# Attention and mixture of experts on one core: the orders of TensorE and ScalarE behind the last first scores, written out by hand

## The chip, the cores and the metric

The kernel runs on one core of a Trainium2 chip. The metric is the device time of one execution in microseconds (us), the lower the better. Before the change it is 196.55 us, the median of three runs (196.53 to 196.87).

## The reference

Eight sequences of 256 tokens with 128 features pass one block: attention with 16 heads of 8 features and a sliding window of 128 tokens, a residual and a layer norm, then a mixture of 8 experts of which each token uses its best two, a residual and a second layer norm.

```python
qkv = x @ w_qkv.T                        # x: (8, 256, 128); 16 heads, D = 8
att = einsum('bhqd,bhkd->bhqk', q, k) / sqrt(8)
att = where((j <= i) & (j >= i - 127), att, -inf); att = softmax(att)
out = einsum('bhqk,bhkd->bhqd', att, v) @ w_out.T
x1 = layernorm(x + out)
probs = softmax(x1 @ router_w); top_p, top_e = top_k(probs, 2)
y = sum over the two experts e of p_e * (gelu(x1 @ w_in[e] + b_in[e]) @ w_out[e] + b_out[e])
result = layernorm(x1 + y)
```

## The kernel before

Five engines each run a program of their own in order, and wait for one another by counting semaphores: a `wait_ge` stands ahead of the instruction that needs it, and everything behind it on that engine waits too.

**Attention.** Batch `b` (0 to 7) has 16 heads in 8 pairs. TensorE computes first scores (`scores`), from which VectorE takes the maximum of each row. The maxima are split in three bf16 parts, turned (`turn_max`), copied by ScalarE (`copy_max`) and put as extra rows under the stacked q by a DMA. Then TensorE computes the scores a second time, turned (keys on the partitions) and with the maximum subtracted: `turned_scores(b, p)` for pair `p`. ScalarE takes `exponentials(b, p)` of them, GpSimd masks two pairs (a quad `g`) at once with two selects (`mask_probs`, lines 443 and 445), and TensorE weighs the values with them (`weigh_values(b, g)`, called the product of quad g here). `turned_scores` has two places to write in turn (`pair_banks`), so a pair waits for the exponential of the pair before last. When four quads are done, ScalarE copies the output (`copy_output`), TensorE turns it (`turn_output`), VectorE divides by the sums (`normalise`), TensorE turns it back (`turn_attention`), ScalarE copies it (`copy_attention`), TensorE projects it (`project_out`), VectorE adds the residual and takes statistics, GpSimd makes the reciprocal deviation (`first_deviation`, lines 435 and 437), VectorE normalises (`first_norm`, line 770), and TensorE turns the result (`turn_x1`) and computes the router's logits (`route_logits`).

**What sets the order.** One loop over slots runs on each engine. In a slot each engine asks for every kind of work whether its turn has come (`batch_at(slot, offset)`, `pair_at`, `quad_at`). First scores end with slot 63 (`LAST_S1`); `turned_scores` lags them by 11 slots (`S2`), the products by 15 (`PV`). So slots 64 to 74 hold the turned scores of batch 6, pairs 5 to 7, and of batch 7. In these slots TensorE also issues `keep_warm(2, hid_bank[0])`, two products of zeros, 512 columns wide, that nobody reads: in slots 65 to 72, so 16 in all. VectorE has its own loop over the same slots, with this order behind the first scores: `normalise(5)`, `route_shift` (665), `split_weights` (784, 786), the residual, statistics and moments of batch 5, the routing of the first half of the tokens in stages (674 to 694) with `first_norm(5)` (770) in the middle, `split_x1(5)`, `normalise(6)` (743).

**Mixture of experts.** Tokens go in four chunks of 512. For each chunk and expert TensorE computes `first_layer(c, e)` (three products, 1173), ScalarE the gelu (`gelu`, 594), TensorE `second_layer(c, e)` (1187), and VectorE adds the share with its gate (860). `first_layer(0, 0)` stands in slot 73 already; gelu needs another activation table than the exponential, so ScalarE loads it between `exponentials(7, 7)` and `gelu(0, 0)`.

Of the kernel before, what the change touches and what calls it, by code (L numbers as in the profile page):

```python
# [12 lines left out]
B = 8  # L13
# [13 lines left out]
QUADS = H // 4  # L27
# [18 lines left out]
LAST_S1, LAST_S2 = 8 * B - 1, 8 * B - 1 + S2  # L46
# [34 lines left out]
def attention_moe(nc, x_t, x, wqkv_t, wout_t, router_w, w_in, b_in_t, w_out, b_out, out):  # L81
    scratch = nc.dram_tensor("scratch", [2, 2, ROWS, 2, PAIRS * T], BF16, kind="Internal").ap()

    with ExitStack() as ctx:  # L84
# [394 lines left out]
        def _(act):  # L479
# [71 lines left out]
            def route_exponentials(tiles, k):  # L551

                act.wait_ge(route_shifted, k)
                nc.scalar.activation(route[1][:, tiles, :], route[0][:, tiles, :], ACT.Exp).then_inc(route_exp, 1)
# [18 lines left out]
            for n in range(PICKED):  # L573
                take_even(n)

            for slot in range(LAST_S2 + 1):
                n = pair_at(slot)
                if n is not None:
                    exponentials(*n)
                for offset, piece in ((TURN_MAX, copy_max), (TURN_ATTN, copy_attention), (PROJECT_QK, take_top), (PROJECT_QK + 1, take_middle),  # L580
                                      (VALUES, pad_v), (COPY_O, copy_output), (TURN_X1, copy_x1), (LOGITS, copy_logits)):
                    b = batch_at(slot, offset)
                    if b is not None:
                        piece(b)
                if slot == LAST_S1 + 3:
                    route_exponentials(EARLY, 1)

            def gelu(c, e):

# [381 lines left out]
        def _(pe):  # L971
            mm = nc.tensor.matmul

            def keep_warm(count, bank=o_bank[:, :]):

                for _ in range(count):
                    mm(bank, idle_rows[:, 0:P], idle_rows[:, :], start=True, stop=True)
# [186 lines left out]
            def first_layer(c, e):  # L1164

                n = c * NX + e
                if n == 1:
                    pe.wait_ge(exp_done, B * PAIRS - 1)
                if n >= 2:
                    pe.wait_ge(gelu_done, n - 1)  # L1170
                cols = slice(c * CH, (c + 1) * CH)
                for i, (w, xx) in enumerate(((w_in_lo, x1_hi), (w_in_hi, x1_lo), (w_in_hi, x1_hi))):
                    last = mm(hid_bank[e % 2], w[:, e, :], xx[:, cols], start=i == 0, stop=i == 2)  # L1173
                last.then_inc(hid_ready, 1)
# [50 lines left out]
                pick_pair(n)  # L1225
            pe.wait_ge(consts_ready, 7)

            for slot in range(LAST_S2 + 1):
                n = pair_at(slot)
                if n is not None:  # L1230
                    turned_scores(*n)
                elif 0 < slot < S2:
                    keep_warm(2)
                n = jobs_at(slot)
                if n is not None:
                    scores(*n)

                b = batch_at(slot, TURN_MAX)
                if b is not None:
                    turn_max(b)  # L1240
                b = batch_at(slot, TURN_ATTN)
                if b is not None:
                    if b == 0:
                        pe.wait_ge(out_w_loaded, 16)
                    turn_attention(b)
                b = batch_at(slot, PROJECT_OUT)
                if b is not None:
                    project_out(b)
                b = batch_at(slot, PROJECT_QK)
                if b is not None:  # L1250
                    if b % 2 == 0:
                        pe.wait_ge(x_t_loaded[1 + b // 2], 16)
                    if b == 2:
                        pe.wait_ge(part_low, 2)
                    elif b < 5:
                        pe.wait_ge(max_copied, b - 2)
                    else:
                        pe.wait_ge(attn_copied, b - 4)
                    project_qk(b)
                b = batch_at(slot, VALUES)  # L1260
                if b is not None:
                    project_v(b)
                b = batch_at(slot, TURN_X1)
                if b is not None:
                    turn_x1(b)
                b = batch_at(slot, TURN_O)
                if b is not None:
                    turn_output(b)
                b = batch_at(slot, LOGITS)
                if b is not None:  # L1270
                    if b == 0:
                        pe.wait_ge(router_loaded, 16)
                    route_logits(b)
                n = quad_at(slot)
                if n is not None:
                    weigh_values(*n)
                b = batch_at(slot, PROJECT_QK + 1)
                if b is not None:
                    subtract_top(b)
                if slot > LAST_S1 + 1 and slot < LAST_S2 - 1:  # L1280
                    keep_warm(2, hid_bank[0])
                if slot == LAST_S2 - 1:
                    pe.wait_ge(w_lo_done, 1)
                    first_layer(0, 0)

            weigh_values(B - 1, QUADS - 2)
            first_layer(0, 1)
            second_layer(0, 0)
            weigh_values(B - 1, QUADS - 1)
            unit(0, 2)  # L1290
            turn_x1(B - 2)
            unit(0, 3)
# [71 lines left out]
```

## Time and profile before

| | |
|---|---|
| median of three runs | 196.55 us (196.53 to 196.87) |
| profiled execution | 196.5 us, of which the span of the trace 194.8 |
| TensorE busy | 169.4 us (87%) |
| VectorE busy | 154.8 us (79%) |
| ScalarE busy | 114.6 us (59%) |
| GpSimd busy | 84.1 us (43%) |
| granted TensorE clock, mean | 0.994 |

The profiled execution took 1.7 us more than its span, which is what lies around the first and the last instruction. Times in the trace count from the span's start. In its rows PE is TensorE (PEld its weight loads), DVE VectorE, ACT ScalarE, POOL GpSimd. A product's busy time goes on past the start of the next one, since they are pipelined; what a piece of work takes from TensorE is the distance from its start to the start of the next piece. The same holds for ScalarE and VectorE by some tens of ns. Slots 64 to 74 lie between 110.6 and 127.4 us.

### The profile page before, as it was taken

The numbers are of one execution on the slowest core, as the hardware profiler recorded it, in microseconds if no ns is written. First come the engines' busy times: TensorE is split into PE (matmuls) and PEld (weight loads), VectorE is DVE, ScalarE is ACT, GpSimd is POOL, SyncE is SP. The second block draws the span as 40 slices with busy tenths as digits, with TensorE's granted clock in tenths as the row PEclk, the third lists the DMA queues.
The fourth block names the chain that finished last, engine by engine and source line by source line (L and its number), as shares of the span: only waits on it lengthen the run. The fifth ranks groups of instructions, "written<-read, shape, count | busy, mean of one in ns | idle before, by whom it ended". The sixth has DMA issues, their size and how long they took to land. (4 is left out here: it accounts for less than half of the span.)

```text
span 194.8 us, 6184 instructions
## 1 busy us (share of the span) xinstructions
PE 169.4 (87%) x2450; PEld 121.5 (62%) x2460; DVE 154.8 (79%) x468; ACT 114.6 (59%) x216; POOL 84.1 (43%) x157
## 2 busy tenths in 40 slices
PE   7579887988989989889999899989999979999950
PEld 3354454655656656556656544558988869999950
DVE  6985959669598698697988999635798869898793
ACT  4542056687686766876857757564353784564720
POOL 7960006556563655746738366561043002603003
PEclk9999999999999999999999999999999999999997
DMA  5589594194780882955901000000000000020011
GB/s 142 148 232 222 168 242 132 53 212 125 158 226 11 176 206 72 214 160 110 218 13 57 2 8 0 3 0 0 5 0 0 3 27 27 0 59 0 3 53 54
DMA packets 23127, 17.25 MB, mean 89 GB/s; under 512 B 1827, under 2 KB 21179, under 8 KB 23099
## 3 DMA queue, kind: packets, MB, share of 16 engines
q1 hardware_dynamic: 23099, 16.87, 35.2%
q8 instruction: 19, 0.31, 0.7%
q14 instruction: 9, 0.07, 0.1%
HBM read 9.35 MB, written 7.34 MB: 86 GB/s over the span
## 5 line engine op out<-in xcount | busy, mean ns | idle before, releaser
L486 ACT ACTIVATE probs<-st 128x768 f32<-128x768 f32 x59 | 47.9, 811 | 23.8 <-PE st L1067 20.6
L443 POOL TENSOR_SCALAR_AFFINE_SELECT probs<-probs 128x1024 f32<-128x1024 f32 x32 | 35.1, 1097 | 57.4 <-ACT probs L486 57.3
L713 DVE TENSOR_REDUCE max_parts<-score_banks 128x2 f32<-128x384 f32 x64 | 32.6, 550 | 4.6 <-PE score_banks L1041 4.2
L594 ACT ACTIVATE hid<-score_banks,b_in_sb 128x512 f32<-128x512 f32 x32 | 21.9, 687 | 21.0 <-PE score_banks L1173 20.9
L716 DVE TENSOR_REDUCE max_parts<-score_banks 128x4 f32<-128x512 f32 x32 | 20.6, 686 | 13.6 <-PE score_banks L1041 13.6
L1067 PE MATMUL st<-stack 51*64 51x256 bf16 (+1 forms) x472 | 21.2, 254 | 6.2 <-ACT probs L486 5.7
L1030 PE MATMUL score_banks<-edges,ident_bf 64*64 64x256 bf16 (+1 forms) x192 | 19.0, 296 | 4.5 <-DVE max_parts L713 3.4
L1089 PE MATMUL o_bank<-probs,v 128*32 128x256 f32 x256 | 20.4, 391 | 0.0
L445 POOL TENSOR_SCALAR_AFFINE_SELECT probs<-probs 128x512 f32<-128x512 f32 x32 | 20.3, 634 | 0.0
L1067 PEld LDWEIGHTS st<-stack 51*64 51x64 bf16 (+1 forms) x472 | 8.6, 104 | 18.7 <-ACT probs L486 11.8
L860 DVE SCALAR_TENSOR_TENSOR x_rows<-st,gate,x_rows 128x128 f32<-128x128 f32 x64 | 18.1, 344 | 2.4 <-PE st L1187 2.0
L1041 PE MATMUL score_banks<-stack 48*64 48x192 bf16 (+2 forms) x512 | 19.1, 224 | 0.0
L1187 PEld LDWEIGHTS st<-w_out_sb,hid 128*128 128x128 f32 x128 | 16.6, 191 | 2.9 <-ACT hid L594 1.7
L1187 PE MATMUL st<-w_out_sb,hid 128*128 128x128 f32 x128 | 17.0, 276 | 1.3 <-ACT hid L594 1.3
L1173 PE MATMUL score_banks<-x_hi,w_in_lo 128*128 128x512 f32 x32 | 15.4, 480 | 0.0
L1030 PEld LDWEIGHTS score_banks<-edges,ident_bf 64*64 64x64 bf16 x192 | 7.5, 105 | 10.3 <-DVE max_parts L713 4.7
L1041 PEld LDWEIGHTS score_banks<-stack 48*64 48x64 bf16 x512 | 13.9, 107 | 0.0
L1091 PE MATMUL o_bank<-probs,v 128*32 128x128 f32 x256 | 12.9, 273 | 0.0
L1173 PE MATMUL score_banks<-x_hi,w_in_hi 128*128 128x512 f32 x32 | 12.6, 393 | 0.0
L1173 PE MATMUL score_banks<-x_lo,w_in_hi 128*128 128x512 f32 x32 | 12.6, 393 | 0.0
L468 POOL TENSOR_SCALAR var<-moments 128x2 f32<-128x2 f32 x8 | 1.7, 216 | 24.1 <-DVE moments L908 24.1
L1091 PEld LDWEIGHTS o_bank<-probs,v 128*32 128x32 f32 x256 | 8.3, 110 | 5.5
(136 smaller groups left out, 331.2 us busy)
## 6 DMA issues: line engine op xcount, KB each, us to landing
stack<-scratch SPq DMA_DIRECT2D x28, 192.0 KB, 4.0
scratch<-parts SPq DMA_DIRECT2D x16, 192.0 KB, 4.0
scratch<-parts SPq DMA_DIRECT2D x24, 128.0 KB, 3.8
x_rows<-x SPq DMA_DIRECT2D x4, 256.0 KB, 5.6
out<-y_sb SPq DMA_DIRECT2D x8, 128.0 KB, 1.8
x_t_sb<-x_t SPq DMA_DIRECT2D x3, 256.0 KB, 4.8
w_in_sb<-w_in SPq DMA_DIRECT2D x1, 512.0 KB, 5.8
w_out_sb<-w_out SPq DMA_DIRECT2D x1, 512.0 KB, 7.9
```

The costliest lines, as they stand in the source:

```text
L443: pool.affine_select(out=own, in_=own, compare_op=ALU.is_ge, fill=0.0, base=0, pattern=[[0, 2], [0, 4], [1, P]], channel_multiplier=-1).th ...
L486: nc.scalar.activation(probs[g][:, :, two, :].rearrange("p k j c -> p j k c"), pair_banks(PAIRS * b + p)[:, :, 0:3 * P].rearrange("p j (k ...
L594: nc.scalar.activation(hid[e % 2][:, :], hid_bank[e % 2], ACT.Gelu_apprx_tanh, bias=b_in_sb[:, e:e + 1]).then_inc(gelu_done, 1)
L713: nc.vector.tensor_reduce(top[:, 1, r, pair:pair + 2], bank[:, 0:384].rearrange("p (h c) -> p h c", h=2), X_AXIS, ALU.max, negate=True).th ...
L716: nc.vector.tensor_reduce(top[:, 0, r, pair:pair + 4], bank[:, :].rearrange("p (h c) -> p h c", h=4), X_AXIS, ALU.max, negate=True).then_i ...
L1030: mm(at, ident_bf[rows, 64 * r:64 * r + 64], mask, start=True, stop=True)
L1041: last = mm(bank[lo:lo + 64, i * width:i * width + keys.stop - keys.start], q[rows, pair + i, queries], k[rows, pair + i, keys], start=Fal ...
L1067: last = mm(to[cols, r, kt * T:kt * P + T], k[rows, p, at:at + 64], q[rows, p, kt * P:T], start=b > 0 or kt == 0, stop=b > 0, skip_group_c ...
L1089: last = mm(o_bank[rows, t * T:(t + 1) * T], v, probs[g][:, 0:2, j, :], start=s == 0, stop=s == 1, skip_group_check=True)
L1091: last = mm(o_bank[rows, t * T + P:(t + 1) * T], v, probs[g][:, 2, j, :], start=False, stop=s == 1, skip_group_check=True)
L1173: last = mm(hid_bank[e % 2], w[:, e, :], xx[:, cols], start=i == 0, stop=i == 2)
L1187: last = mm(y_bank[e % 4][:, i * E:(i + 1) * E], hid[e % 2][:, i * P:(i + 1) * P], w_out_sb[:, e, :], start=True, stop=True)
```

## The change

The loops of TensorE and of ScalarE end with slot 63, and the work of slots 64 to 74 stands written out, each call by hand. VectorE, GpSimd and the DMA queue keep their loops and their order. `late` is batch 6, `last` is batch 7.

```diff
--- before.py
+++ after.py
@@ -573,7 +573,7 @@
             for n in range(PICKED):
                 take_even(n)
 
-            for slot in range(LAST_S2 + 1):
+            for slot in range(LAST_S1 + 1):
                 n = pair_at(slot)
                 if n is not None:
                     exponentials(*n)
@@ -582,8 +582,27 @@
                     b = batch_at(slot, offset)
                     if b is not None:
                         piece(b)
-                if slot == LAST_S1 + 3:
-                    route_exponentials(EARLY, 1)
+
+            late, last = B - 2, B - 1
+            exponentials(late, 5)
+            copy_max(last)
+            exponentials(late, 6)
+            copy_attention(late - 1)
+            exponentials(late, 7)
+            route_exponentials(EARLY, 1)
+            exponentials(last, 0)
+            exponentials(last, 1)
+            pad_v(last)
+            copy_output(late)
+            exponentials(last, 2)
+            exponentials(last, 3)
+            copy_x1(late - 1)
+            exponentials(last, 4)
+            copy_logits(late - 1)
+            exponentials(last, 5)
+            copy_attention(late)
+            exponentials(last, 6)
+            exponentials(last, 7)
 
             def gelu(c, e):
 
@@ -1225,7 +1244,7 @@
                 pick_pair(n)
             pe.wait_ge(consts_ready, 7)
 
-            for slot in range(LAST_S2 + 1):
+            for slot in range(LAST_S1 + 1):
                 n = pair_at(slot)
                 if n is not None:
                     turned_scores(*n)
@@ -1277,16 +1296,40 @@
                 b = batch_at(slot, PROJECT_QK + 1)
                 if b is not None:
                     subtract_top(b)
-                if slot > LAST_S1 + 1 and slot < LAST_S2 - 1:
-                    keep_warm(2, hid_bank[0])
-                if slot == LAST_S2 - 1:
-                    pe.wait_ge(w_lo_done, 1)
-                    first_layer(0, 0)
-
-            weigh_values(B - 1, QUADS - 2)
+
+            late, last = B - 2, B - 1
+            turned_scores(late, 5)
+            turn_max(last)
+            turned_scores(late, 6)
+            weigh_values(late, 1)
+            turn_attention(late - 1)
+            turned_scores(late, 7)
+            weigh_values(late, 2)
+            project_out(late - 1)
+            keep_warm(2, hid_bank[0])
+            turned_scores(last, 0)
+            turned_scores(last, 1)
+            project_v(last)
+            weigh_values(late, 3)
+            turned_scores(last, 2)
+            turned_scores(last, 3)
+            turn_x1(late - 1)
+            turn_output(late)
+            turned_scores(last, 4)
+            route_logits(late - 1)
+            weigh_values(last, 0)
+            turned_scores(last, 5)
+            turn_attention(late)
+            turned_scores(last, 6)
+            weigh_values(last, 1)
+            project_out(late)
+            turned_scores(last, 7)
+            weigh_values(last, 2)
+            pe.wait_ge(w_lo_done, 1)
+            first_layer(0, 0)
             first_layer(0, 1)
             second_layer(0, 0)
-            weigh_values(B - 1, QUADS - 1)
+            weigh_values(last, 3)
             unit(0, 2)
             turn_x1(B - 2)
             unit(0, 3)
```

TensorE, at the turned scores of pairs 6 and 7 of batch 6 (1067 turned scores, 1138 `turn_attention(5)`, 1089 and 1091 the product of a quad, 977 the idle products, 1145 `project_out(5)`). Before:

```order
L1067 MATMUL score_banks<-stack 64x256 [waits maxima]
L1067 MATMUL score_banks<-stack 64x256 x3
L1067 MATMUL score_banks<-stack 64x128 x4
L1138 MATMUL misc<-ident,attn 128x128 [waits normed,max_copied]
L1138 MATMUL misc<-ident,attn 128x128
L1089 MATMUL o_bank<-probs,v 32x256 [waits masked]
L1089 MATMUL o_bank<-probs,v 32x256 x3
L1091 MATMUL o_bank<-probs,v 32x128 x4
L977 MATMUL score_banks<-idle_rows 128x512 x2
L1067 MATMUL st<-stack 64x256 [waits exp_done]
L1067 MATMUL st<-stack 64x256 x3
L1067 MATMUL st<-stack 64x128 x4
```

Now, with line numbers 19 higher:

```order
L1086 MATMUL score_banks<-stack 64x256 [waits maxima]
L1086 MATMUL score_banks<-stack 64x256 x3
L1086 MATMUL score_banks<-stack 64x128 x4
L1108 MATMUL o_bank<-probs,v 32x256 [waits masked]
L1108 MATMUL o_bank<-probs,v 32x256 x3
L1110 MATMUL o_bank<-probs,v 32x128 x4
L1157 MATMUL misc<-ident,attn 128x128 [waits normed,max_copied]
L1157 MATMUL misc<-ident,attn 128x128
L1086 MATMUL st<-stack 64x256 [waits exp_done]
L1086 MATMUL st<-stack 64x256 x3
L1086 MATMUL st<-stack 64x128 x4
L1108 MATMUL o_bank<-probs,v 32x256 [waits masked]
```

The product of quad 1 has moved ahead of `turn_attention(5)`, the turned scores of pair 7 stand ahead of the next product (of quad 2), and two pairs of idle products have become one.

TensorE, further on, from the turned scores of batch 7, pair 3 (1154 is `turn_x1(5)`, 1127 `turn_output(6)`, 1161 `route_logits(5)`). Before:

```order
L1067 MATMUL st<-stack 64x256 [waits exp_done]
L1067 MATMUL st<-stack 64x256 x3
L1067 MATMUL st<-stack 64x128 x4
L1154 MATMUL misc<-ident,x_rows 128x128 [waits x1_done]
L1154 MATMUL misc<-ident,x_rows 128x128
L977 MATMUL score_banks<-idle_rows 128x512 x2
L1067 MATMUL score_banks<-stack 64x256 [waits exp_done]
L1067 MATMUL score_banks<-stack 64x256 x3
L1067 MATMUL score_banks<-stack 64x128 x4
L1127 MATMUL misc<-ident,o_t 128x128 [waits o_copied,v_padded]
L1127 MATMUL misc<-ident,o_t 128x128 x3
L1161 MATMUL misc<-router_sb,x_t 128x8 [waits x1_copied]
```

Now:

```order
L1086 MATMUL st<-stack 64x256 [waits exp_done]
L1086 MATMUL st<-stack 64x256 x3
L1086 MATMUL st<-stack 64x128 x4
L1173 MATMUL misc<-ident,x_rows 128x128 [waits x1_done]
L1173 MATMUL misc<-ident,x_rows 128x128
L1146 MATMUL misc<-ident,o_t 128x128 [waits o_copied,v_padded]
L1146 MATMUL misc<-ident,o_t 128x128 x3
L1086 MATMUL score_banks<-stack 64x256 [waits exp_done]
L1086 MATMUL score_banks<-stack 64x256 x3
L1086 MATMUL score_banks<-stack 64x128 x4
L1180 MATMUL misc<-router_sb,x_t 128x8 [waits x1_copied]
L1180 MATMUL misc<-router_sb,x_t 128x8
```

`turn_output(6)` has moved from behind the turned scores of pair 4 to ahead of them, and the idle products have gone. Ahead of this piece the product of batch 6, quad 3, has moved in front of the turned scores of batch 7, pairs 2 and 3, which now stand back to back. Behind it `turn_attention(6)` moves from behind the turned scores of pair 6 to ahead of them, `project_out(6)` from behind those of pair 7 to ahead of them, and `first_layer(0, 0)` from ahead of them to behind the product of batch 7, quad 2.

On ScalarE two copies move: `copy_output(6)` from behind `exponentials(7, 3)` to ahead of `exponentials(7, 2)`, `copy_attention(6)` from behind `exponentials(7, 6)` to ahead of it. The routing's exponential (554) keeps its place behind `exponentials(6, 7)`.

## Rows read from the trace of the kernel before

**Rows 1.** Windows; after the window: its length, busy us and instructions by engine, clock, DMA:

```profile
115.00:125.00 10.00, 9.45 (x130) 4.63 (x130) 9.18 (x32) 6.29 (x15) 6.04 (x8) 1.00 0.00 0
130.40:188.00 57.60, 56.05 (x416) 50.55 (x416) 47.32 (x192) 32.36 (x56) 11.56 (x31) 1.00 0.04 13
188.00:194.80 6.80, 0.00 (x0) 0.00 (x0) 3.57 (x17) 0.00 (x0) 1.81 (x4) 0.83 0.20 57
```

**Rows 2.** Timeline of TensorE, 111 to 117: start, busy, line, tiles, [idle before]:

```profile
111.16 0.36 PE L1067 MATMUL score_banks<-stack 51*64 51x256 bf16 x8
112.20 0.44 PE L1138 MATMUL misc<-ident,attn 128*128 128x128 f32 x2 [0.68 <-ACT max_t L508]
112.56 0.64 PE L1089 MATMUL o_bank<-probs,v 128*32 128x256 f32 x8
...
113.89 0.36 PE L1067 MATMUL st<-stack 51*64 51x256 bf16 x8
...
115.54 0.64 PE L1089 MATMUL o_bank<-probs,v 128*32 128x256 f32 x8
...
116.33 0.60 PE L977 MATMUL score_banks<-idle_rows 128*128 128x512 bf16 x2
```

**Rows 3.** Timeline of ScalarE, the exponential of batch 6, pair 7:

```profile
114.30 0.81 ACT L486 ACTIVATE probs<-st 128x768 f32<-128x768 f32 x1 [1.18 <-PE st L1067]
```

**Rows 4.** Timeline of VectorE, 114 to 125:

```profile
114.20 1.22 DVE L786 TENSOR_TENSOR w_in_lo<-w_in_sb,w_in_hi 128x1024 fp32r<-128x1024 f32 x1
...
116.31 0.25 DVE L764 BATCH_NORM_AGGREGATE moments<-stats 128x2 f32<-128x6 f32 x2
...
118.26 1.07 DVE L678 TENSOR_TENSOR route<-route,row_stat 128x64 f32<-128x64 f32 x1
119.37 0.81 DVE L770 TENSOR_SCALAR x_rows<-resid,moments,rstd 128x128 f32<-128x128 f32 x2
...
121.37 0.93 DVE L678 TENSOR_TENSOR route<-route,row_stat 128x64 f32<-128x64 f32 x1
122.34 0.55 DVE L693 TENSOR_TENSOR route<-route 128x64 f32<-128x64 f32 x1
...
124.25 0.62 DVE L743 TENSOR_TENSOR attn<-misc,inv_sum 128x64 f32<-128x64 f32 x4
```

**Rows 5.** Timeline of GpSimd, 112 to 122:

```profile
112.98 0.64 POOL L445 TENSOR_SCALAR_AFFINE_SELECT probs<-probs 128x512 f32<-128x512 f32 x1
115.18 1.20 POOL L443 TENSOR_SCALAR_AFFINE_SELECT probs<-probs 128x1024 f32<-128x1024 f32 x1 [1.56 <-ACT probs L486]
...
116.94 0.21 POOL L435 TENSOR_SCALAR var_eps<-moments 128x2 f32<-128x2 f32 x1
117.23 0.70 POOL L437 TENSOR_TENSOR rstd<-var_eps,half_power 128x2 f32<-128x2 f32 x1
118.16 1.09 POOL L443 TENSOR_SCALAR_AFFINE_SELECT probs<-probs 128x1024 f32<-128x1024 f32 x1 [0.23 <-ACT probs L486]
...
121.13 1.09 POOL L443 TENSOR_SCALAR_AFFINE_SELECT probs<-probs 128x1024 f32<-128x1024 f32 x1 [1.29 <-ACT probs L486]
```

**Rows 6.** Lines 678 and 770 over the whole run; min/median/max ns of one:

```profile
L678 DVE TENSOR_TENSOR route<-route,row_stat x4: 217/578/1073, 118.3 to 161.2; 128x64 f32<-128x64 f32 x4
L770 DVE TENSOR_SCALAR x_rows<-resid,moments,rstd x16: 333/432/668, 55.1 to 143.3; 128x128 f32<-128x128 f32 x16
```

**Rows 7.** Timeline of TensorE, 125 to 131:

```profile
125.05 0.44 PE L1138 MATMUL misc<-ident,attn 128*128 128x128 f32 x2
...
127.10 0.36 PE L1067 MATMUL st<-stack 51*64 51x256 bf16 x8
127.39 0.71 PE L1145 MATMUL misc<-wout_sb,attn_t 128*128 128x128 f32 x4
...
130.38 1.16 PE L1187 MATMUL score_banks<-w_out_sb,hid 128*128 128x128 f32 x8 [0.60 <-ACT hid L594]
```

**Rows 8.** Timeline of TensorE at the start of the run:

```profile
1.24 3.60 PE L977 MATMUL o_bank<-idle_rows 128*128 128x512 bf16 x8 [1.24 <-DVE idle_rows L810]
```

## The prediction, as it stood before the changed kernel ran

> **What bounds the kernel now.** I read the windows first, for where each engine is busy [rows 1]. The reader is to see two regimes. From 130.40 to 188.00 TensorE is busy for 56.05 of 57.60 us: the mixture of experts runs at its pace, and behind it only the last norm and the store are left. So whatever moves the start of `second_layer(0, 0)` at 130.38 [rows 7] moves the end by as much. Ahead of it, from 115 to 125, TensorE is busy for 9.46 of 10 us, but VectorE too, for 9.18 [rows 1]. Part of TensorE's time are the idle products; VectorE has nothing of the kind.
>
> Then I read the timelines of that stretch, for what VectorE does there. It runs without a wait from 114.20 to the end of `normalise(6)` at 124.25 + 0.62 = 124.87 [rows 4]. `turn_attention(6)` on TensorE starts at 125.05 [rows 7], 0.18 behind it. Everything up to `second_layer(0, 0)` hangs on that one: 130.38 - 125.05 = 5.33 us of turned scores, a product, the last exponential, a table load and a gelu. So the pacer of the changed stretch is VectorE, with TensorE 0.1 us behind: a completion is seen some 0.07 us later (the exponential of [rows 3] ends at 115.11, the select behind it starts at 115.18 [rows 5]).
>
> Third, what VectorE's time is made of. Some of its instructions last longer than others of their line: 678 takes 0.217 us at the least and 1.073 at the most, 770 0.333 and 0.668 [rows 6]. The long ones lie under GpSimd's selects: 678 at 118.26 lasts until 119.33, the select at 118.16 until 119.25; 678 at 121.37 lasts until 122.30, the select at 121.13 until 122.22 [rows 4, 5]. Both end 0.08 behind it, which is less than their own 0.22: they wait until about 0.15 before the select's end and get in between its two halves. The costs from 115.42 to 124.87 are 0.85 and 0.71 (678), 0.55 - 0.22 = 0.33 (693), and 0.2 (770, whose pair takes 0.81 instead of 0.6): 2.1 us in all.
>
> **The change part by part.** (1) 14 of 16 idle products go. Two take at most 0.60 us [rows 2], so 14 take up to 4.2. If TensorE paced the stretch that would be the gain. It does not, so by itself this is worth the 0.18 - 0.07, some 0.12 us, that `turn_attention(6)` starts later than VectorE allows.
>
> (2) The turned scores of batch 6, pair 7, move from 113.89 [rows 2] to the front. Those of pair 6 start at 111.16 as before and take 0.29, the product of quad 1 takes 0.79 (115.54 to 116.33) and ends at 112.24, `turn_attention(5)` takes 0.36 (112.20 to 112.56) [rows 2], so they start at 112.60, 1.29 earlier. The exponential follows 0.41 later as now (113.89 to 114.30 [rows 2, 3]), at 113.0, and the select of quad 3 after it at 113.9 instead of 115.18 [rows 5]. It runs until 115.0.
>
> (3) That select now lies on `split_weights`. The difference of the weights (786), a 1024 wide operation with both inputs in SBUF like 678, starts at 114.20 and takes 1.22 [rows 4]; today the select comes when it is nearly done, and it is the select that lasts 1.20 instead of 1.09 [rows 5]. Now it finds the select running. By the behaviour of 678 it runs from 115.0 - 0.15 and ends at 116.1, against 115.42: 0.65 late. If the cast ahead of it (784, which ends where 786 starts) holds the select back, another 0.15. I take 0.7. Bounds: 0, if 786 doesn't wait as 678 does, and 1.4, if both halves of the select pass first (0.8, and 0.64 for the second half [rows 5]).
>
> No row here shows whether a cast can hold back a select. The Trainium skill (SBUF — State Buffer, section Who interferes with whom) says that a VectorE operation with two SBUF inputs, or a cast in a two-port mode, and a GpSimd operation that reads SBUF exclude each other for a whole instruction, whoever came first going on. By that rule the select starts at 114.1, 786 waits for its full end at 115.2 and ends at 116.4, and the sum below would be 197.3 instead of 197.0; the trace agrees on who waits, but its 678 ends only 0.08 behind the select.
>
> (4) VectorE's order behind it is unchanged, so statistics and moments of batch 5 end at 116.56 + 0.7 = 117.26 [rows 4]. GpSimd makes the deviation from them: 0.07, 0.30 (116.94 to 117.23) and 0.70 [rows 5], until 118.35. Then come the selects of batch 7. Its pairs 0 to 3 are ahead of time now (the select of quad 2 ends at 113.62 as now [rows 5]; its product 0.79, `project_out(5)` and two idle products bring the first two turned scores to 115.6 and 115.9, values and a product the next two to 117.9 and 118.2; with 0.41 to each exponential and 0.81 for it, and the copies of ScalarE between, the exponentials of pairs 1 and 3 are done at about 117.6 and 120.05), so quad 0 is selected from 118.4 to 120.1 and quad 1 right behind, from 120.15 to 121.85, instead of 118.16 and 121.13 [rows 5]. VectorE meets them with 676, 678 and the pair 770: 676 loses 0.85, 678 0.1, the first 770 0.8 (it starts just behind the begin of quad 1's select), the second 0.35. That is 2.1, as much as today, at other places; 678's second time, 693 and the split of x1 are clear of selects. `normalise(6)` ends 0.7 late, at 125.55.
>
> (5) TensorE meanwhile stands. `turn_x1(5)` needs the norm of line 770, which ends at 121.9, and the turned scores of pair 3 are issued by 118.5: 3.4 us without a product, where the idle products used to be. From there to the turned scores of pair 5 lie six pieces of work: two turned scores at 0.29, a product at 0.79, and three turns or projections, between 0.36 and 0.71 each by their nearest rows [rows 2, 7]: 2.5 to 3.5 us, done by 124.4 to 125.4. `turn_attention(6)` starts at 125.6, with `turn_output(6)` and the logits, moved ahead of it, hidden in VectorE's lateness (without that cover they cost up to 0.9).
>
> (6) Behind `turn_attention(6)` before: 0.36, product 0.79 and `first_layer(0, 0)` with the rest, 0.90, then the turned scores of pair 7, 127.10 - 125.05 = 2.05 us after it [rows 7]. Now: 0.36, turned scores of pair 6 0.29, product 0.79, `project_out(6)` up to 0.71 [rows 7]: 2.05 to 2.15. The same. `first_layer(0, 0)` and `(0, 1)`, 1.8 us, go behind the turned scores, under the last exponential and the table load, where TensorE waited 0.60 us [rows 7]; they fill that. The copies moved on ScalarE come ahead of exponentials that wait for TensorE anyway.
>
> **Sum.** 0.7 (786) + 0 (other meetings) - 0.12 (TensorE's lag) + 0 = 0.55 later at `second_layer(0, 0)`, and I take 0.5 for the cheap ends of the steps. The profiled execution took 196.5 us (194.8 and 1.7 around it), 0.05 under the median: 197.0 us. With 0.6 to 0.8 in (3) and 0.25 either way in (4), 196.75 to 197.4. Measurement tells a change from none at about 0.2%, 0.4 us.
>
> **The rivals.**
>
> *A, faster: VectorE escapes the selects.* What speaks for it: selects that come earlier may fall on reductions and on operations that read PSUM, which don't wait (the two moments at 116.31 took 0.25 although a select ran [rows 4, 5]). If none of 676, 678 and 770 waits, `normalise(6)` ends 2.1 earlier than in my sum, at 123.45, and the end comes 1.5 us earlier than today: 195.0. It is faster from the point where more than 0.6 of the 2.1 is saved. Against it: GpSimd works through quads 0 and 1 without a gap for 3.4 us, and all four instructions lie there. Chance 0.20, spread over 195.0 to 196.1.
>
> *B, no change: the delay is absorbed.* 786 is late but 0.3 to 0.6 comes back, since one select meets 677 instead of 676, or quad 1's select comes behind the pair 770 (it takes 0.3 us of lateness of its exponentials). 196.2 to 196.9. Chance 0.22.
>
> *C, my forecast*, 196.75 to 197.4, chance 0.48.
>
> *D, the clock falls.* TensorE stands for 3.4 us at 118.5 and works about half of the time around it. Today the granted clock is 1.00 from 115 to 188; after the last product, before 188.0, it stays up and falls only at about 192.5 (mean 0.83 over the last 6.8 us) [rows 1], over 4 us later. At the start of the run eight idle products take 3.60 us, 0.45 each, against 0.30 later [rows 2, 8]; that is the slow level of the clock, and it lasted that long. If it fell to 1.2 GHz at 121.9, the work of (5) and (6) would run at half speed for at least as long, which loses half of 3.6, 1.8 us, and TensorE has at most 1.2 us of waiting for VectorE there to pay from: 0.6 more than my forecast at the least, up to 2 if the clock comes back late: 197.6 to 199. Chance 0.10.
>
> The Trainium skill (TensorE: Matmul & The Clock Gate, section HAM oscillation — how this bites in real kernels) warns of just such gaps between bursts; no row of this trace shows a fall inside the run.
>
> **How the numbers follow.** Slower by over 0.2%: D, and C but for its lowest tenth, 0.54. Same: B with what falls between, 0.25. Faster: A and the low edge of B, 0.21. The range leaves out the far half of A and of D: 195.9 to 197.8.
>
> **What would show it.** In the changed profile: the select of batch 6, quad 3, at 113.9, and 786 lasting 1.9 us instead of 1.22 (right: step 3); two quads of selects back to back from 118.4 with 676 and 770 long; TensorE waiting for x_rows of line 770 some 3.4 us; `turn_attention(6)` waiting for VectorE, at 125.6; `second_layer(0, 0)` at 130.9; from there to the end 64.4 us as now. If 786 lasts 1.22, or `normalise(6)` ends before 124.9, the forecast is wrong on the fast side; a granted clock under 1.00 between 118 and 130 means D.

## The result, and the profile after

The changed kernel is slower: 200.09 us, the median of four runs (199.07 to 200.81), against 196.56 before (196.53 to 196.87). The ratio is 1.0172, with a 95% interval of 1.0126 to 1.0218. The profiled execution took 200.09 us, its span 198.3; the prediction was 197.0, at most 197.8.

The page of the changed kernel, busy tenths and the granted clock in 40 slices of 4.96 us:

```profile
PE   7589887989989989899988883999999979999960
...
DVE  6985958678698696897988999324889869998793
...
PEclk9999999999999999999999996589999999999997
```

The third row is what is new: the clock digits read 6, 5 and 8 in slices 25 to 27, where the page of the kernel before has a 9 in each. The windows, two us each, show when (columns as in [rows 1]: TensorE's busy us come first behind the length, and the clock is the third number from the right):

```profile
116.00:118.00 2.00, 1.48 (x28) 0.94 (x20) 1.83 (x10) 1.96 (x6) 1.19 (x3) 1.00 0.00 0
118.00:120.00 2.00, 0.57 (x21) 0.31 (x16) 1.86 (x5) 1.84 (x4) 2.00 (x3) 1.00 0.00 0
120.00:122.00 2.00, 0.00 (x0) 0.00 (x0) 1.96 (x4) 0.18 (x1) 1.85 (x3) 0.66 0.00 0
122.00:124.00 2.00, 1.94 (x15) 1.33 (x15) 1.73 (x10) 0.38 (x1) 0.00 (x0) 0.50 0.00 0
124.00:126.00 2.00, 2.00 (x20) 1.52 (x20) 1.60 (x8) 0.99 (x2) 0.00 (x0) 0.50 0.00 0
...
128.00:130.00 2.00, 2.00 (x21) 1.16 (x20) 0.00 (x0) 0.87 (x2) 1.53 (x2) 0.50 0.00 0
130.00:132.00 2.00, 2.00 (x28) 1.15 (x28) 1.16 (x5) 0.89 (x2) 0.03 (x1) 0.78 0.00 0
132.00:134.00 2.00, 1.45 (x7) 0.84 (x6) 0.00 (x0) 1.99 (x3) 1.92 (x4) 1.00 0.00 0
```

TensorE is busy for 0.57 us of 118 to 120 and for nothing of 120 to 122. The clock is 1.00 until then, 0.66 on the mean of 120 to 122, 0.50 until 130 and 0.78 in the next two: it fell at about 120.7 and came back at about 130.9, so for 10.2 us it was at the lower of its two levels, 1.2 instead of 2.4 GHz. It came back after TensorE had been busy for 8.8 us almost without a gap, from 122.06 on.

TensorE's timeline has the same story (`turn_x1(5)` is the row of 122.06, `turn_attention(6)` that of 126.85, the last turned scores 130.52, `second_layer(0, 0)` 133.96):

```profile
118.23 0.34 PE L1086 MATMUL st<-stack 51*64 51x256 bf16 x8
122.06 0.69 PE L1173 MATMUL misc<-ident,x_rows 128*128 128x128 f32 x2 [3.50 <-DVE x_rows L789]
...
126.85 0.69 PE L1157 MATMUL misc<-ident,attn 128*128 128x128 f32 x2
...
130.52 0.52 PE L1086 MATMUL st<-stack 51*64 51x256 bf16 x8
...
133.96 1.16 PE L1206 MATMUL score_banks<-w_out_sb,hid 128*128 128x128 f32 x8 [0.55 <-ACT hid L613]
```

`second_layer(0, 0)` comes at 133.96 instead of 130.38 [rows 7], 3.58 late, and the span is 3.5 longer: behind it nothing was gained or lost. The row at 122.06 waits 3.50 us for the norm; such a time in which TensorE has nothing to issue is called a stop below. VectorE's rows (805 is 786 of before, 695 is 676, 789 is 770, 762 is 743), from its timeline:

```profile
114.23 1.99 DVE L805 TENSOR_TENSOR w_in_lo<-w_in_sb,w_in_hi 128x1024 fp32r<-128x1024 f32 x1
...
118.51 1.15 DVE L695 TENSOR_TENSOR route<-route,rank_w 128x64 f32<-128x64 f32 x1
...
120.29 1.72 DVE L789 TENSOR_SCALAR x_rows<-resid,moments,rstd 128x128 f32<-128x128 f32 x2
...
125.05 0.61 DVE L762 TENSOR_TENSOR attn<-misc,inv_sum 128x64 f32<-128x64 f32 x4
```

GpSimd's timeline beside them, the last select of batch 6 and quads 0 and 1 of batch 7:

```profile
113.93 1.22 POOL L443 TENSOR_SCALAR_AFFINE_SELECT probs<-probs 128x1024 f32<-128x1024 f32 x1 [0.28 <-ACT probs L486]
...
118.50 1.09 POOL L443 TENSOR_SCALAR_AFFINE_SELECT probs<-probs 128x1024 f32<-128x1024 f32 x1
...
120.25 1.09 POOL L443 TENSOR_SCALAR_AFFINE_SELECT probs<-probs 128x1024 f32<-128x1024 f32 x1
```

The difference of the weights lasts 1.99 us instead of 1.22, under the select that starts at 113.93; the norm's pair lasts 1.72 instead of 0.81 [rows 4], under the selects from 118.50 to 121.9. `normalise(6)` ends at 125.05 + 0.61 = 125.66 instead of 124.87.

### The profile page after: what moved, and what is told of

Same layout as the page of the kernel before. It is cut to its first block and busy times, and to the rows that moved or that the text cites. A ratio compares the mean times of both kernels' runs of the same rounds, so it can differ in the third digit from the quotient of the medians.

```text
span 198.3 us, 6166 instructions
## 1 busy us (share of the span) xinstructions
PE 171.2 (86%) x2446; PEld 122.7 (62%) x2446; DVE 155.5 (78%) x468; ACT 114.3 (58%) x216; POOL 85.2 (43%) x157
## 5 line engine op out<-in xcount | busy, mean ns | idle before, releaser
L1108 PE MATMUL o_bank<-probs,v 128*32 128x256 f32 x256 | 21.3, 406 | 0.7 <-POOL probs L445 0.7
L445 POOL TENSOR_SCALAR_AFFINE_SELECT probs<-probs 128x512 f32<-128x512 f32 x32 | 21.3, 664 | 0.0
L1110 PE MATMUL o_bank<-probs,v 128*32 128x128 f32 x256 | 13.4, 282 | 0.0
```

What stands on the lines that cost most here:

```text
L445: pool.affine_select(out=other, in_=other, compare_op=ALU.is_gt, fill=0.0, base=0, pattern=[[0, 4], [-1, P]], channel_multiplier=1).then_i ...
L1108: last = mm(o_bank[rows, t * T:(t + 1) * T], v, probs[g][:, 0:2, j, :], start=s == 0, stop=s == 1, skip_group_check=True)
L1110: last = mm(o_bank[rows, t * T + P:(t + 1) * T], v, probs[g][:, 2, j, :], start=False, stop=s == 1, skip_group_check=True)
```

## The experiments

Two theories stood against each other at first. Theory 1: two costs add, VectorE's lateness (by the walk 0.55) and the fallen clock (the rest, 3.0). Theory 2: the new order itself costs the time, and the clock is a companion. A third question was what let the clock fall, the missing idle products alone (in any order) or the new order with them (theory 3).

A note on comparing traces. The runs of one kernel lie mostly in two groups some 0.6 us apart (17 runs of before: 196.5 to 196.9 and 197.0 to 197.2), and the traces start in two ways. The first projection shows it, here from TensorE's timeline of the changed kernel:

```profile
4.62 1.03 PE L1002 MATMUL misc<-x_t_sb,wqkv_sb 128*128 128x256 f32 x4
```

And the same row of e1_fill:

```profile
4.62 1.86 PE L1002 MATMUL misc<-x_t_sb,wqkv_sb 128*128 128x256 f32 x4
```

It takes 1.03 us in one and 1.86 in the other, and in the second everything behind starts 0.57 us later (`turn_max(7)` at 111.54 instead of 110.97). That the clock reached its upper level later in the second is an inference from these durations: the profile's clock reads 1.00 there in both. No kernel was traced in both ways, but among the kernels that held the clock the traced run lies in the upper group where it starts like the second (e1_fill, e4_split_fill, e8_last_first) and in the lower one where it starts like the first (before, e2_late67, e9_before_last_first). Times of a trace of the second kind are given below with 0.6 taken off (0.57 for e1_fill), and called shifted.

Each ratio is against the runs of before in the same set: their median was 196.55 beside e1_fill, e2_late67, e3_before_noidle and e5_split, 196.96 beside e4_split_fill, e6_fill4 and e7_late67_bare, and 196.99 beside the last two, since the groups were filled differently. So medians of different sets differ by up to 0.4 us that no kernel made.

| run | median us | ratio to before, 95% | `second_layer(0, 0)` |
|---|---|---|---|
| e1_fill | 197.81 | 1.0051 (1.0036 to 1.0066) | 131.15 shifted |
| e2_late67 | 196.62 | 1.0015 (0.9992 to 1.0039) | 130.48 |
| e3_before_noidle | 198.40 | 1.0080 (1.0058 to 1.0103) | 133.14, of it 1.13 from an earlier stretch |
| e5_split | 197.95 | 1.0069 (1.0051 to 1.0087) | 131.7 shifted |
| e6_fill4 | 199.03 | 1.0120 (1.0100 to 1.0139) | 132.96 |
| e7_late67_bare | 198.93 | 1.0111 (1.0092 to 1.0130) | 132.05 shifted |
| e4_split_fill | 196.38 | 0.9976 (0.9965 to 0.9987) | 130.0 shifted |
| e8_last_first | 195.57 | 0.9930 (0.9911 to 0.9949) | 129.3 shifted |
| e9_before_last_first | 196.36 | 0.9985 (0.9971 to 0.9999) | 130.30 |

**e1_fill: the stop filled with idle products.**

```diff
             turned_scores(last, 3)
+            keep_warm(12, hid_bank[0])
             turn_x1(late - 1)
```

> The changed kernel with 12 idle products put back in one place, between the turned scores of batch 7, pair 3, and turn_x1(5), where TensorE stood from 118.6 to 122.1 us; nothing else. Theory 1 (the fallen clock costs 3.0 us of the 3.5, VectorE's lateness the other 0.55): granted clock 1.00 through the stretch, second_layer(0, 0) at 130.9, 196.9 to 197.2 us, ratio to before about 1.0025. Theory 2 (the new order itself costs the time, the clock only makes it look worse): turn_x1(5) at 122 as in the changed kernel and still 198.5 us or more.

Measured: 197.81 us, clock 1.00 from 111 to 188. TensorE's timeline (times of this trace, unshifted):

```profile
119.30 2.54 PE L996 MATMUL score_banks<-idle_rows 128*128 128x512 bf16 x11 [0.16 <-issue]
122.64 0.44 PE L1173 MATMUL misc<-ident,x_rows 128*128 128x128 f32 x2 [0.81 <-DVE x_rows L789]
...
131.72 1.16 PE L1206 MATMUL score_banks<-w_out_sb,hid 128*128 128x128 f32 x8 [0.55 <-ACT hid L613]
```

VectorE's row of the weights in the same trace:

```profile
114.80 1.99 DVE L805 TENSOR_TENSOR w_in_lo<-w_in_sb,w_in_hi 128x1024 fp32r<-128x1024 f32 x1
```

The idle products take the place of the stop (their row holds 11 of the 12), `turn_x1(5)` comes at 122.07 shifted, as in the changed kernel, and `second_layer(0, 0)` at 131.15 shifted instead of 133.96. The only difference between the two kernels are products that nobody reads, so 2.8 of the 3.58 us are the clock's, and theory 2 falls. What is left, 0.77 over before, is somewhat more than the 0.55 of the walk; the ratio, 1.0051, is above the 1.0025 that was expected. Part of that is that more of its runs fell into the upper group; its fastest run, 197.24, is 0.77 above the fastest of before, 196.47.

**e2_late67: the exponential of batch 6, pair 7, back to its later place.**

```diff
             turn_attention(late - 1)
-            turned_scores(late, 7)
             weigh_values(late, 2)
+            turned_scores(late, 7)
             project_out(late - 1)
...
             turned_scores(last, 3)
+            keep_warm(12, hid_bank[0])
             turn_x1(late - 1)
```

> As e1_fill, and the turned scores of batch 6, pair 7, behind the product of quad 2 instead of ahead of it, so that its exponential comes at 114.9 and the select of quad 3 at 115.8, clear of the split of the weights. If the lateness of VectorE comes from that one meeting: the weights' difference takes 1.22 us again instead of 1.99, normalise(6) ends 0.6 us earlier than in e1_fill, at about 125.0, second_layer(0, 0) at 130.3, 196.4 to 196.7 us. If VectorE is late for another reason: as e1_fill.

Measured: 196.62 us. VectorE's timeline:

```profile
114.21 1.22 DVE L805 TENSOR_TENSOR w_in_lo<-w_in_sb,w_in_hi 128x1024 fp32r<-128x1024 f32 x1
...
124.39 0.61 DVE L762 TENSOR_TENSOR attn<-misc,inv_sum 128x64 f32<-128x64 f32 x4
```

And `second_layer(0, 0)` in TensorE's:

```profile
130.48 1.16 PE L1206 MATMUL score_banks<-w_out_sb,hid 128*128 128x128 f32 x8 [0.55 <-ACT hid L613]
```

The weights' difference takes 1.22 again, `normalise(6)` ends at 125.00 and `second_layer(0, 0)` comes 0.67 ahead of e1_fill. VectorE still loses 2.1 us to the other selects, as before and as in e1_fill, only in other instructions. So the one meeting of a VectorE operation with a select is what made the new order slower than the old one at full clock; without it no difference between the two orders is left that these runs can tell. Three of its twelve runs were above 197.2 (up to 198.76), and in the two slowest, 198.58 and 198.76, the mean clock of the run was 0.984 and 0.985, against 0.992 to 0.995 in the nine runs of 196.6 to 196.7. That points to a fall of the clock in two of twelve runs in spite of the 12 idle products, but neither was traced, and the mean clock alone does not show it (e4_split_fill has 0.987 in a run of 196.05, one of its fastest).

**e3_before_noidle: the old order without the idle products.**

```diff
-                if slot > LAST_S1 + 1 and slot < LAST_S2 - 1:
-                    keep_warm(2, hid_bank[0])
```

> The kernel before, in its old order, with only the 16 idle products of slots 65 to 72 taken out. Theory 1: by the walk with the durations of before, TensorE then stands 2.5 us ahead of turn_x1(5) and 1.2 ahead of turn_attention(6); at full clock the time would be within 0.2 us of before (196.4 to 196.6), since VectorE paces. If the clock falls (a stop of 2.1 us was enough in the changed kernel) 198 to 200 us. Theory 3 (the order is what lets the clock fall, not the missing idle products): clock 1.00 and 196.5 us.

Measured: 198.40 us (197.95 to 199.23). Windows of the profiled execution:

```profile
58.00:60.00 2.00, 2.00 (x27) 1.23 (x28) 1.87 (x10) 0.75 (x2) 0.29 (x1) 0.67 0.05 13
60.00:62.00 2.00, 2.00 (x44) 1.44 (x44) 1.02 (x4) 1.24 (x3) 0.68 (x1) 0.50 0.00 0
...
120.00:122.00 2.00, 0.11 (x1) 0.11 (x2) 1.96 (x4) 1.08 (x2) 2.00 (x4) 1.00 0.00 0
122.00:124.00 2.00, 2.00 (x26) 1.44 (x30) 1.76 (x8) 1.36 (x3) 0.34 (x1) 0.88 0.00 0
124.00:126.00 2.00, 1.77 (x32) 0.77 (x24) 1.84 (x9) 0.49 (x1) 0.00 (x0) 0.50 0.00 0
...
130.00:132.00 2.00, 2.00 (x29) 1.31 (x22) 0.95 (x4) 1.70 (x2) 0.84 (x1) 0.91 0.00 0
```

The clock falls in this stretch in the old order too (0.88, 0.50, 0.91 from 122 on), behind a stop of 2.16 us ahead of `turn_x1(5)`: at about 123.5, when TensorE had been at work again for 1.6 us. Theory 3 is out: the idle products held the clock, not the order.

The profiled execution shows a second fall, 58.7 to 62.1, in code that is the same as before; TensorE was busy for 1.48 of 2 us just ahead of it. In the same window of the kernel before it was busy for 1.46 of 2 us, and the clock stayed at 1.00. So nearly the same work can come with a fall or without one. Everything behind this fall starts 1.13 us later than before (`turn_max(7)` at 112.07 instead of 110.94). Without these 1.13 `second_layer(0, 0)` would have come at 132.0, 1.6 late, and the execution of 199.23 would be near the 197.95 and 198.02 of the two fastest, which were not traced.

**e5_split: VectorE's split of the weights moved out of its path.**

```diff
-                if slot == LAST_S1 + 2:
+                if slot == LAST_S1 + 10:
                     split_weights()
```

> The changed kernel with one call of VectorE moved: split_weights goes from slot 65 to slot 73, behind normalise(6), where VectorE waited 3.3 us before. No idle products put back. Walk at full clock: the norm of line 770 ends at 119.7 instead of 121.9, TensorE stands 1.7 us ahead of turn_x1(5) and 2.1 ahead of turn_attention(6), normalise(6) ends at 124.4, second_layer(0, 0) at 129.65: 195.7 to 196.0 us, if the clock holds. If it falls with two stops of about 2 us: 197.5 to 199.

Measured: 197.95 us. `turn_x1(5)` comes at 119.8 shifted, as walked, and the stops are 1.80 and 1.53 us, but the clock falls all the same, as the windows show:

```profile
118.60:122.00 3.40, 1.60 (x19) 1.29 (x18) 3.23 (x8) 2.65 (x6) 2.80 (x4) 1.00 0.00 0
122.00:132.00 10.00, 8.23 (x85) 4.35 (x85) 6.75 (x20) 5.09 (x8) 4.10 (x6) 0.66 0.01 2
```

0.66 over ten us is 6.8 us at the lower level. The stop ahead of `turn_x1(5)` ended at 120.40, and the clock fell only at about 122.4, with TensorE busy for the whole 2 us between. At full clock the walk had `second_layer(0, 0)` at 129.65, and it came at 131.7.

**e6_fill4 and e7_late67_bare: each cause half undone.**

```diff
             turned_scores(last, 3)
+            keep_warm(4, hid_bank[0])
             turn_x1(late - 1)
```

> The changed kernel with only 4 idle products in the gap instead of 12: TensorE works until 119.6 and then stands for 2.5 us. If any work in the gap keeps the clock: as e1_fill, 197.3 us. If the stop itself lets it fall, as with the 2.2 us of e3_before_noidle: clock below 1.00 for a part of 119 to 131 in most runs, 198 to 200 us, less than the changed kernel's 200.1 at the most.

> The changed kernel with the turned scores of batch 6, pair 7, behind the product of quad 2 as in e2_late67, but no idle products put back. VectorE is in time then (weights' difference 1.22 us), so what is left against before is the clock alone: normalise(6) ends at 125.0, TensorE stands some 3 us ahead of turn_x1(5). If the two causes add: 2.9 us over e2_late67, about 199.5 us, against 200.1 for the changed kernel. If the clock falls only because VectorE is late: 196.6 us.

e7_late67_bare is e2_late67 without its `keep_warm(12, ...)`. The window of e6_fill4:

```profile
122.00:132.00 10.00, 9.57 (x100) 5.50 (x101) 4.53 (x22) 5.16 (x8) 2.71 (x3) 0.66 0.01 2
```

And its TensorE's timeline:

```profile
122.12 0.44 PE L1173 MATMUL misc<-ident,x_rows 128*128 128x128 f32 x2 [2.53 <-DVE x_rows L789]
...
123.22 0.61 PE L1180 MATMUL misc<-router_sb,x_t 128*128 128x8 f32 x4
123.76 0.90 PE L1108 MATMUL o_bank<-probs,v 128*32 128x256 f32 x8
```

The window of e7_late67_bare, and the row behind its stop:

```profile
122.00:132.00 10.00, 9.14 (x96) 5.17 (x96) 4.53 (x19) 5.07 (x8) 3.84 (x6) 0.66 0.01 2
```

```profile
121.10 0.44 PE L1173 MATMUL misc<-ident,x_rows 128*128 128x128 f32 x2 [1.65 <-DVE x_rows L789]
```

In both the clock is down for 6.8 us (0.66 over ten). e6_fill4 takes 199.03: four idle products (their row is not shown) leave a stop of 2.53 us out of 3.50, and the clock falls all the same, but not in the stop. The turns at 122.12 still take 0.44 and the logits at 123.22 0.61, as in e1_fill; the product at 123.76 takes 0.90 instead of 0.64, since the clock fell at about 124.0, 1.9 us after the stop.

e7_late67_bare takes 198.93; against the runs of before beside each, it is 1.11% slower and e2_late67 0.15%, so 1.9 us lie between them (1.6 between the two traces). Its stop ahead of `turn_x1(5)` is 1.65 us, and the clock fell at about 122.4, 1.3 us behind it. The clock's price is there without VectorE's lateness, so the causes are two. It is smaller than the 2.9 that was expected, and e6_fill4 shows that the length of the slow stretch accounts for most of that: with VectorE as late as in e1_fill, its `second_layer(0, 0)` comes 1.8 us behind that of e1_fill for 6.8 us at the lower level, where the changed kernel's comes 2.8 behind for 10.2.

**e4_split_fill and e8_last_first: a version that is faster than both kernels.** e4_split_fill is e5_split with 6 idle products ahead of `turn_x1(5)` and 6 ahead of `turn_attention(6)`. e8_last_first adds to it:

```diff
             turned_scores(last, 6)
+            turned_scores(last, 7)
             weigh_values(last, 1)
             project_out(late)
-            turned_scores(last, 7)
-            weigh_values(last, 2)
             pe.wait_ge(w_lo_done, 1)
             first_layer(0, 0)
+            weigh_values(last, 2)
```

> The changed kernel with split_weights of VectorE behind normalise(6) and 12 idle products put back: 6 ahead of turn_x1(5), 6 ahead of turn_attention(6), the two places where TensorE stood 1.8 and 1.5 us in e5_split. Theory 1 (at full clock what is left is VectorE's path, which this shortens): clock 1.00 through the stretch, turn_x1(5) at 119.8, turn_attention(6) at 124.5, second_layer(0, 0) at 129.7 (0.7 ahead of before), 195.8 to 196.1 us, ratio about 0.997. Rival: the second half of the split meets the select of batch 7, quad 2, w_lo comes too late for first_layer(0, 0), or the idle products themselves get in the way: 196.5 us or more.

> e4_split_fill with the turned scores of batch 7, pair 7, right behind those of pair 6, and the product of quad 1, project_out(6), first_layer(0, 0) and the product of quad 2 behind them. Walk: turned scores of pair 7 at 125.1 instead of 126.5, table load done 1.2 us before TensorE is ready, so TensorE's work is the bound and second_layer(0, 0) comes at 129.45, 0.2 ahead of e4_split_fill: 195.8 to 196.1 us at the common start of the runs, ratio to before about 0.996. Rival: the wait for the gelu stays and it is as e4_split_fill, 0.9976.

e4_split_fill took 196.38, 0.24% under before, where 0.3% was expected. In its trace `second_layer(0, 0)` is 0.4 us ahead of before and not 0.7: `turn_attention(6)` came at 125.29, 124.7 shifted, 0.2 later than walked, and TensorE still waited 0.54 for the gelu. e8_last_first took 195.57, 0.7% under before: 0.9 us between the two by these ratios and 0.75 by the traces (130.62 and 129.87), where 0.2 was expected. TensorE's timeline of e8_last_first (unshifted):

```profile
125.26 0.41 PE L1157 MATMUL misc<-ident,attn 128*128 128x128 f32 x2 [0.68 <-DVE attn L762]
...
125.79 0.34 PE L1086 MATMUL st<-stack 51*64 51x256 bf16 x8
...
129.87 1.05 PE L1206 MATMUL score_banks<-w_out_sb,hid 128*128 128x128 f32 x8
```

And ScalarE's, where 126.78 is the last exponential and 127.60 the table load:

```profile
126.78 0.80 ACT L486 ACTIVATE probs<-st 128x768 f32<-128x768 f32 x1
127.60 1.28 ACT L613 ACT_TABLE_LOAD   x1
128.90 0.69 ACT L613 ACTIVATE hid<-score_banks,b_in_sb 128x512 f32<-128x512 f32 x1
```

The gelu is done at 129.59 and TensorE comes to `second_layer(0, 0)` at 129.87 without a wait. From `turn_attention(6)` to it are 4.61 us, where before had 5.33 [rows 7]. The expectation, 129.45 less the 124.5 of e4_split_fill's walk, leaves about 4.95. Two turned scores back to back take 0.19 for the first one and not 0.29, which is 0.1 of the difference; the rest was not traced to a piece of work.

**e9_before_last_first: the same idea in the old order.**

```diff
-                if n is not None:
+                if n is not None and slot != LAST_S2 - 1:
                     weigh_values(*n)
...
-                if slot == LAST_S2 - 1:
+                if slot == LAST_S2:
+                    weigh_values(B - 1, 1)
                     pe.wait_ge(w_lo_done, 1)
```

> The kernel before with one thing moved: the product of batch 7, quad 1, and first_layer(0, 0) go from slot 73 behind the turned scores of pair 7 and project_out(6) in slot 74. All 16 idle products stay. If the wait of TensorE ahead of second_layer(0, 0) (0.60 us) comes from the late last exponential: turned scores of pair 7 at 125.4 instead of 127.1, the wait goes, second_layer(0, 0) at 129.7 to 129.9, 196.0 us, ratio 0.997. If not: 1.000.

Measured: 196.36 us, a ratio of 0.9985 (0.9971 to 0.9999), half of what was expected and barely clear of none; in the trace `second_layer(0, 0)` comes at 130.30, 0.08 ahead of before and not 0.5 to 0.7. The wait of 0.60 us ahead of `second_layer(0, 0)` went, and one of 0.59 came ahead of `project_out(6)`, which now waits for `copy_attention(6)` behind an exponential on ScalarE. The changed kernel's order on ScalarE, with that copy ahead of the exponential, is one thing that e8_last_first has in addition here; the split of the weights out of VectorE's path is the other.

## Why the prediction was wrong

**The step that failed is rival D, in its chance and in its price.** The sum has no term for the clock: it stands at nothing, and the stop of 3.4 us that step 5 worked out stands there at no cost. Rival D was given 0.10, and 197.6 to 199. The fall is there in the trace of the changed kernel, the mean clocks of its other three runs (0.963 to 0.977, against 0.994 before) point to it there too, and all four took longer than 199. Three statements under it were off. First, that the clock "falls only at about 192.5, over 4 us later" was read as the patience of the clock with a stop. In the changed kernel it had fallen 2.1 us into the stop (118.57 to 120.7), and in e3_before_noidle, e5_split, e6_fill4 and e7_late67_bare it fell 1.3 to 2.0 us behind stops of 2.16, 1.80, 2.53 and 1.65 us. The one row on the end of the run could not carry that weight; it said how long it took in one case, not how long it takes at the least. At the end of the other ten traced runs the same delay is 1.8 to 4.8 us. Second, the time at the lower level was taken from the start of the run, 3.6 us; it was 10.2 in the changed kernel, of which TensorE was busy for all but the first 1.4, and 6.8 in four experiments. (The start is also misread in one number: 0.30 for an idle product at the upper level is half of a pair's busy time with its tail. The 11 in 2.54 us of e1_fill take 0.23 each, half of the 0.45 at the start.) Third, the price: it was argued that TensorE had 1.2 us of waiting to pay from. `turn_attention(6)` came at 126.85 and not 125.6, 1.19 behind `normalise(6)`, so that cover was used up (at full clock it would have been 0.96, the wait ahead of `turn_attention(6)` in e1_fill), and the rest of the path ran at the lower level up to 130.9: `turn_attention(6)` to `second_layer(0, 0)` took 7.11 us instead of 5.33. 1.19 and 1.78 make 2.97, less the 0.15 by which TensorE starts behind VectorE in e1_fill as well: the 2.8 of e1_fill.

**What was right.** Steps 1 to 5, at full clock, nearly to the tenth:

| step | predicted | changed kernel |
|---|---|---|
| select of batch 6, quad 3 | 113.9 | 113.93 |
| weights' difference | 1.9 us | 1.99 |
| selects of batch 7, quads 0 and 1 | 118.4, 120.15 | 118.50, 120.25 |
| 770's pair ends | 121.9 | 122.0 |
| stop ahead of `turn_x1(5)` | 3.4 us | 3.50 |
| `normalise(6)` ends | 125.55 | 125.66 |

So VectorE paced the stretch and the removed idle products gave no time back: they became a stop. Step 3 named the one meeting that made VectorE late, and e2_late67 against e1_fill shows it: 0.67 us for one operation. Step 4, that the other meetings cost as much as before, held within 0.1: 0.79 of lateness, of which 0.77 came with the weights' difference. Rival A, that VectorE escapes the selects, and rival B, that the delay is absorbed, are out by these rows.

**Step 6 and the sum.** At full clock the cost was 0.77 (e1_fill) against 0.55 in the sum (whose terms, 0.7 less 0.12, make 0.58; and its 9.46 us of TensorE from 115 to 125 are 9.45 in [rows 1], on which nothing hangs). `normalise(6)` accounts for 0.79 of lateness and not 0.7; and the 0.12 of TensorE's lag did not come back, since `turn_attention(6)` starts 0.15 behind VectorE in e1_fill too, where before had 0.18. That is where the small gain of step 1 went. The forecast of the direction, slower, rested on VectorE's lateness, and that is 0.8 of the 3.6 us; the other 2.8 were in a rival that should have had the larger chance.

**What was cited.** The Trainium skill's warning of gaps between bursts (TensorE: Matmul & The Clock Gate, section HAM oscillation — how this bites in real kernels) was cited under rival D with "no row of this trace shows a fall inside the run". The runs bear it out: the traces of all five kernels without enough idle products (the changed one, e3, e5, e6, e7) show a fall in or behind a stop of 1.65 to 3.50 us. The Trainium skill's rule on the shared SBUF port (SBUF — State Buffer, section Who interferes with whom) holds as to who waits: the select of 113.93 lasts 1.22 instead of 1.09 behind the cast, and the weights' difference waits for it. But by the full end of the select it would have ended at 116.4; it ended at 116.22, between that and the 116.1 taken from 678. The select's second half waited for it in turn (1.61 us from 115.10 on, instead of 0.63).

## What to carry to other kernels

A wait that fillers cover is not free time: before taking fillers out, find what paces the stretch, and how long TensorE will stand with nothing issued. Look for the fall of the clock behind the stop too, and not only in it. Here products that nobody reads held the clock at its upper level, and every version that left a stop of 1.65 us or more ahead of `turn_x1(5)` took 1.4 to 3.5 us more than before. How many fillers that stop needs was tried only at 4 (too few) and 12 (enough in every trace, and perhaps not in two runs of e2_late67); where the stop was shorter, 6 and 6 held the clock (e4_split_fill, e8_last_first).

Work that is moved forward on one engine moves its followers too. A select that came 1.25 us sooner landed on a VectorE operation that then waited for it, and cost 0.67 us, more than the move could bring. Look at what each moved completion releases, and on what it falls.

The new order paid only when the pacer's own path was shortened first (the split of the weights out of it), the stops were filled, and the last exponential was issued as early as its inputs allow: 195.57 against 196.99 us in the same set of runs.

## What the runs showed of the hardware that was not expected

The clock fell 2.1 us into a stop in one kernel, and in four others only when TensorE had been busy again for 1.3 to 2.0 us. Behind the last product of a run, where nothing more is issued, it fell after 4.6 us in the kernel before (mean 0.83 over the last 6.8 us [rows 1]), after 1.8 in e6_fill4, after 2.6 in e4_split_fill and after 4.0 to 4.8 in the other eight traces. A single observed delay is no bound.

Once down, it stayed down for 10.2 us in the changed kernel, with TensorE busy for the last 8.8 of them, and for 6.8 in four others, where at most one stop of 0.3 to 1.5 us lay in between; in the one fall at 58.7 (e3_before_noidle) it was 3.4 us. What decides between these lengths is open. The four runs of the changed kernel go the same way, though only the first was traced: mean clock 0.963 to 0.977, 200.81 to 199.07 us.

At the start of a run the first projection takes 1.03 us in some runs and up to 1.97 in others, as if the clock came up at different times, and all that follows is 0.6 us later. For differences of a few tenths of a per cent that is the larger part of the spread.
